# Summing the expert rows of a token block: GpSimd for the first 18 blocks, VectorE for the other 14

## What is computed

```
xn = layernorm(x)
out = x + attention(xn) + ffn(xn)

# ffn: 8 of 64 experts for each token, weighted, and a shared expert
tidx, tw = gate(xn)                      # 8 experts and 8 weights a token
y[t] = sum over k of tw[t,k] * expert[tidx[t,k]](xn[t])
ffn  = y + silu(xn @ Ws_gate) * (xn @ Ws_up) @ Ws_down
```

## Time and profile before

| what | value |
|---|---|
| device time, median of 3 runs | 1333.56 us (1332.71 to 1335.41) |
| profiled execution, its own time | 1338.67 us |
| profiled execution, its span | 1336.9 us |
| mean granted TensorE clock | 0.973 of full speed |
| TensorE (PE) busy | 1255.4 us, 94% |
| VectorE (DVE) busy | 953.3 us, 71% |
| ScalarE (ACT) busy | 861.7 us, 64% |
| GpSimd (POOL) busy | 638.7 us, 48%, nothing from 1000 us on |

### The profile page before, as it was taken

The page is one execution under the profiler, slowest core; times in us unless marked ns, Lnnn a source line. Parts: engine busy times, 40 slices in busy tenths (PEclk is TensorE's granted clock), DMA queues, the critical chain, the costliest instruction groups (busy, mean ns, idle before and its releaser), DMA issues.

```text
span 1336.9 us, 38681 instructions
## 1 busy us (share of the span) xinstructions
PE 1255.4 (94%) x9266; PEld 1182.4 (88%) x9267; DVE 953.3 (71%) x4532; ACT 861.7 (64%) x2383; POOL 638.7 (48%) x747
## 2 busy tenths in 40 slices
PE   4957999999999989999999999999999999999996
PEld 3956999999999979999999999999988999999985
DVE  6776666666666637667676676765559898989897
ACT  2323877777777856556565566566657777777774
POOL 7803777777777726565565665656650000000000
PEclk9678999999999979999999999999999999999998
DMA  8107455544333337777777777775545333333330
GB/s 255 63 1 280 163 185 188 206 163 162 123 118 112 114 120 223 211 233 223 224 232 212 233 226 214 233 215 170 175 139 218 107 106 106 106 109 113 116 119 19
DMA packets 152813, 218.40 MB, mean 163 GB/s; under 512 B 24769, under 2 KB 124866, under 8 KB 147650
## 3 DMA queue, kind: packets, MB, share of 16 engines
q1 hardware_dynamic: 80450, 86.77, 20.4%
q0 software_dynamic: 28800, 86.54, 16.9%
q10 hardware_dynamic: 43520, 44.57, 13.1%
HBM read 113.86 MB, written 103.81 MB: 163 GB/s over the span
## 4 chain that ended last, share of the span: by engine, by line
PE 73%; DVE 12%; issue 6%; DMA 3%; ACTq 2%; ACT 2%; DVEq 1%; SPq 1%
PE psS L951 19%; PE psS L824 10%; PE psT L935 5%; PE psO L960 5%; PE psT L838 4%; PE psM L960 4%; DVE x_all L1604 4%; DMA pr<-slot_rows 2%; PE psQ L771 2%; PE psV L811 2%; PE psV L782 2%; PE psQ L792 2%; PE psT L852 2%; PE psT L851 2%; PE psT L850 1%
## 5 line engine op out<-in xcount | busy, mean ns | idle before, releaser
L951 PEld LDWEIGHTS psS<-sm,wt 128*128 128x128 f32 x2560 | 310.8, 193 | 19.5 <-issue 7.8
L951 PE MATMUL psS<-sm,wt 128*128 128x128 f32 x2560 | 316.6, 277 | 1.7 <-ACT sm L1210 0.7
L636 POOL DMA_INDIRECT slot_rows<-x_out_st,idx_st x256 | 257.0, 1004 | 77.5 <-issue 68.6
L1116 ACT ACTIVATE pr<-sm,nmax 128x192 f32<-128x192 f32 x512 | 205.1, 449 | 54.5 <-DVE nmax L1544 52.7
L824 PE MATMUL psS<-kT,qz 128*128 128x192 f32 x1024 | 225.2, 343 | 10.8 <-DVE qz L1487 8.4
L663 POOL DMA_INDIRECT home_rows<-qz,row_idx x160 | 154.6, 966 | 131.0 <-DVE qz L1637 103.4
L663 POOL DMA_INDIRECT home_rows<-sm,row_idx x160 | 155.3, 971 | 86.4 <-issue 45.0
L1228 ACT COPY wt<-shared_mem 128x512 f32 x320 | 183.4, 627 | 4.8 <-issue 4.8
L1216 ACT ACTIVATE prT<-psS 128x256 f32<-128x256 f32 x160 | 61.6, 385 | 187.7 <-issue 100.0
L824 PEld LDWEIGHTS psS<-kT,qz 128*128 128x128 f32 x1024 | 164.3, 192 | 18.4 <-issue 10.3
L1544 DVE CUSTOM_DVE_ANT_0 sm<-psS,pr 128x192 f32<-128x192 f32 x512 | 162.0, 353 | 18.5 <-issue 14.6
(11 more groups left out here) (283 smaller groups left out, 2492.6 us busy)
## 6 DMA issues: line engine op xcount, KB each, us to landing
shared_mem<-home_rows SPq DMA_DIRECT2D x32, 1024.0 KB, 5.1
pr<-slot_rows ACTq DMA_DIRECT2D x120, 272.0 KB
qz<-slot_rows ACTq DMA_DIRECT2D x40, 272.0 KB
slot_rows<-wt SPq DMA_DIRECT2D x32, 272.0 KB
shared_mem<-in_L_ffn_We_gate SPq DMA_DIRECT2D x64, 128.0 KB
shared_mem<-in_L_ffn_We_up SPq DMA_DIRECT2D x64, 128.0 KB
shared_mem<-in_L_ffn_We_down SPq DMA_DIRECT2D x64, 128.0 KB
x_all<-in_L_attn_x SPq DMA_DIRECT2D x4, 1024.0 KB, 9.1
```

Source lines behind the costliest of these rows:

```text
L636: pool.indirect_dma_start(slot_rows, bass.IndirectOffsetOnAxis(ap=idx_st[:, j, k:k + 1], axis=0), x_out_st[:, j % 2, :], None).then_inc(sc ...
L951: last = mm(psS[:, j % 2, (2 * a + n) * P:(2 * a + n + 1) * P], wt[j % 2][:, a, c, n * F:(n + 1) * F], xsT[:, j % 2, a, c, :], start=(c == ...
L1116: nc.scalar.activation(pr[:, p % 4, par, :], sm[:, p % 4, par, :], ACT.Exp, bias=nmax[:, p % 4, par:par + 1], scale=-1.0).then_inc(probs, 1)
```

## The change

`FIRST` becomes 18, so stage 2 does blocks 0 to 17 and stage 4 does blocks 18 to 31.

Expert rows of blocks 0 to 17 are now summed by GpSimd in stage 4 (`combine_past`), with five instructions a block. The first multiplies the 8 rows (2048 floats a partition) in place by their weights, three additions of 1024, 512 and 256 floats fold them into one, and a last one adds that to `x_all`. All inputs and outputs lie in SBUF. Rows of blocks 18 to 31 stay with VectorE: the body of block i adds the 8 rows of block i itself, one at the end of each step, and in the first body two at the end of each of the last four steps. The `closing` sums are gone. `accumulate` now waits for the block's own expert sum, which the same engine issued before it.

There are five row buffers instead of four, two for GpSimd and three for VectorE. SP's loop is written out: in its step n it waits for VectorE's block n - 1 of this stage, loads VectorE's rows two blocks ahead, tells VectorE of the next block's rows, and then waits for GpSimd's blocks 2n and 2n + 1 in turn, loading GpSimd's next rows and storing the finished block after each.

```diff
-FIRST = NB // 2 + 1
+FIRST = 18
+OWN_ROWS, PAST_ROWS = 3, 2
...
+            def store_past(t):
+                sp.wait_ge(past_combined, t + 1)
+                if t + PAST_ROWS < FIRST:
+                    load_past(t + PAST_ROWS)
+                sp.dma_start(yt[:, t, :], x_all[:, t, :]).then_inc(stored, 16)
+
+            load_past(0)
+            load_own(FIRST)
+            load_past(1)
+            load_own(FIRST + 1)
+            load_own(FIRST + 2)
+            announce_own(FIRST)
+            for n in range(NB - FIRST):
+                t = FIRST + n
+                if n:
+                    sp.wait_ge(combined, n)
+                    if t + 2 < NB:
+                        load_own(t + 2)
+                if t + 1 < NB:
+                    announce_own(t + 1)
+                if n >= 3:
+                    store_own(t - 3)
+                for m in (2 * n, 2 * n + 1):
+                    if m < FIRST:
+                        store_past(m)
...
+            def combine_past(j, t, g):
+                pool.wait_ge(rows_ready[j], 16 * (g + 1))
+                row = rows_in[:, j, :, :]
+                nc.gpsimd.tensor_tensor(row, row, w8[:, t, :].unsqueeze(2).broadcast_to([P, K, D]), ALU.mult).then_inc(past_steps, 1)
+                for n, k in enumerate((K // 2, K // 4, K // 8)):
+                    pool.wait_ge(past_steps, 4 * t + n + 1)
+                    nc.gpsimd.tensor_tensor(row[:, 0:k, :], row[:, 0:k, :], row[:, k:2 * k, :], ALU.add).then_inc(past_steps, 1)
+                pool.wait_ge(past_steps, 4 * t + 4)
+                nc.gpsimd.tensor_tensor(x_all[:, t, :], x_all[:, t, :], row[:, 0, :], ALU.add).then_inc(past_combined, 1)
+
+            pool.wait_ge(weights_kept, 1)
+            pool.wait_ge(acc_done, FIRST)
+            with pool.Fori(0, FIRST // PAST_ROWS) as g:
+                for j in range(PAST_ROWS):
+                    combine_past(j, g * PAST_ROWS + j, g)
...
-                    if closing and s in (1, 2, 5, 7):
-                        n = (1, 2, 5, 7).index(s)
-                        if n == 0:
-                            dve.wait_ge(acc_done, NB - 1)
-                        combine(NB - 2 + n // 2, 2 + n // 2, range(n % 2 * 4, n % 2 * 4 + 4))
-                    if resuming and s >= NPAIR // 2:
-                        for n in range(2):
-                            add_row(i, 4 * s - 2 * NPAIR + n)
-                    if combining:
-                        add_row(i, 2 * s)
...
-                    if resuming and s >= NPAIR // 2:
-                        for n in range(2, 4):
-                            add_row(i, 4 * s - 2 * NPAIR + n)
-                    if combining:
-                        add_row(i, 2 * s + 1)
...
+                    if combining and live and resuming and s >= NPAIR - K // 2:
+                        for k in range(2):
+                            add_row(i, 2 * (s - NPAIR) + K + k)
+                    if combining and live and not resuming:
+                        add_row(i, s)
```

More of the change, by code:

```diff
@@ L118, in build @@
         ring_d = shared_mem[:, RING * 2 * D:RING * WE].rearrange("p (r n) -> p r n", r=RING)
-        rows_in = shared_mem[:, 0:ROWS * K * D].rearrange("p (j k d) -> p j k d", j=ROWS, k=K)
+        rows_in = shared_mem[:].rearrange("p (j k d) -> p j k d", j=OWN_ROWS + PAST_ROWS, k=K)
         gbias = sb("gbias", [P, E])
@@ L340, in build @@
         idx_ready = sem("idx_ready")
-        rows_ready = [sem(f"rows_ready{j}") for j in range(ROWS)]
+        rows_ready = [sem(f"rows_ready{j}") for j in range(OWN_ROWS + PAST_ROWS)]
         rows_landed = sem("rows_landed")
@@ L345, in build @@
         combined = sem("combined")
+        past_steps = sem("past_steps")
+        past_combined = sem("past_combined")
         slot_rows = nc.dram_tensor("slot_rows", (SLOTS + E * P, ROW), F32, kind="Internal").ap()
@@ L469, in _, with load_past, load_own, announce_own @@
                 sp.wait_ge(y_out[j], 32 * (PAIRS // YS))
-            def load_rows(j, t):
+            def load_past(t):
+                sp.dma_start(rows_in[:, t % PAST_ROWS, :, :], home[t]).then_inc(rows_ready[t % PAST_ROWS], 16)
+            def load_own(t):
+                j = PAST_ROWS + t % OWN_ROWS
                 sp.dma_start(rows_in[:, j, :, :], home[t]).then_inc(rows_ready[j], 16)
-            def announce_rows(j, g):
-                sp.wait_ge(rows_ready[j], 16 * (g + 1))
+            def announce_own(t):
+                sp.wait_ge(rows_ready[PAST_ROWS + t % OWN_ROWS], 16 * ((t - FIRST) // OWN_ROWS + 1))
@@ L476, in announce_rows, with store_own @@
                 sp.sem_inc(rows_landed, 1)
-            def store_block(t):
-                sp.wait_ge(combined, t + 1)
+            def store_own(t):
                 sp.wait_ge(acc_done, t + 1)
                 sp.dma_start(yt[:, t, :], x_all[:, t, :]).then_inc(stored, 16)
[L483 to L492, removed]
@@ L493, in _ @@
-            for j in range(ROWS):
-                store_block(NB - ROWS + j)
+            def store_past(t):
[9 more added lines that the diff above has]
+            announce_own(FIRST)
@@ new lines, in _ @@
+            for n in range(NB - FIRST):
[11 more added lines that the diff above has]
+                        store_past(m)
+            for t in range(NB - 3, NB):
+                store_own(t)
@@ L1531, in keep_shared, with accumulate @@
                 v.scalar_tensor_tensor(hs[:], sg[:], 0.5, psQ[:, P:2 * P], ALU.mult, ALU.mult).then_inc(hs_ready, 1)
-            def accumulate(i):
+            def accumulate(i, combining):
                 dve.wait_ge(out_ready, i + 1)
+                if combining:
+                    dve.wait_ge(combined, i - FIRST + 1)
                 v.tensor_tensor(x_all[:, i, :], psV[:, D:2 * D], x_all[:, i, :], ALU.add).then_inc(acc_done, 1)
@@ L1546, in mask_pair, with body @@
                                            nmax[:, p % 4, u:u + 1]).then_inc(masked, 1)
-            def body(i, blk, nth, live=True, tail=True, ahead=True, last_tail=True, combining=False, closing=False, resuming=False):
+            def body(i, blk, nth, live=True, tail=True, ahead=True, last_tail=True, combining=False, resuming=False):
                 if live:
@@ L1553, in body @@
                         mask_pair(i, s, nth)
[L1554 to L1563 removed]
                     if s == 0 and tail and last_tail:
[L1565 removed]
+                        accumulate(i - 2, combining)
                     if s == 1 and live:
@@ L1586, in body, with add_row @@
                         latent_out(i)
-                    if resuming and s >= NPAIR // 2:
-                        for n in range(2, 4):
-                            add_row(i, 4 * s - 2 * NPAIR + n)
-                    if combining:
-                        add_row(i, 2 * s + 1)
[L1594 to L1605, removed]
+                    if combining and live and resuming and s >= NPAIR - K // 2:
[3 more added lines that the diff above has]
+                        add_row(i, s)
+            def add_row(t, k):
+                n = t - FIRST
+                if k == 0:
+                    dve.wait_ge(rows_landed, n + 1)
+                else:
+                    dve.wait_ge(combine_steps, (K - 1) * n + k)
+                row = rows_in[:, bass.ds(PAST_ROWS + t % OWN_ROWS, 1), k, :].rearrange("p a d -> p (a d)")
+                ins = v.scalar_tensor_tensor(x_all[:, t, :], row, w8[:, t, k:k + 1], x_all[:, t, :], ALU.mult, ALU.add)
+                ins.then_inc(combine_steps if k < K - 1 else combined, 1)
             def attention(start, end, combining):
@@ L1614, in attention @@
                     dve.wait_ge(gu_ready, PAIRS)
-                body(start, start % BPS, nth, tail=False, resuming=combining)
+                body(start, start % BPS, nth, tail=False, combining=combining, resuming=combining)
                 body(start + 1, start % BPS + 1, max(nth, 1), last_tail=False, combining=combining)
@@ L1619, in attention @@
                 body(end - 1, (end - 1) % BPS, 2, ahead=False, combining=combining)
[L1620 to L1623, removed]
+                body(end, None, 2, live=False, combining=combining)
+                accumulate(end - 1, combining)
             def make_h(j, u, first):
```

## The result

The changed kernel takes 1402.99 us (median; 1401.31 to 1403.82) against 1334.49 us of the kernel before in the same comparison: 1.0511 times as long, 95% interval 1.0490 to 1.0531. The forecast was 1409 us, in a range of 1355 to 1465. The profiled execution has a span of 1402.0 us and a mean granted TensorE clock of 0.948, against 1336.9 us and 0.973.

A forecast was written before the change was run, and what follows sets the result against it. TensorE was taken to bound stage 2, nearly joined by VectorE in stage 4. Gain -12.8, exclusion +83 and clock +5 us sum to +75 us on 1333.6, so 1409 us, range 1355 to 1465.

The forecast's parts named there:

- The gain, -12.8 us: Stage 4 laid out anew with fewer rows on VectorE, as if GpSimd disturbed nobody: span ends at 1324.1 against 1336.9 us.
- That long instructions shut VectorE out to their end: Stage 4: GpSimd's and VectorE's instructions with two SBUF inputs exclude each other for the whole instruction, even at 4.5 us.
- without exclusion: Rival for stage 4: slack covers exclusion or long instructions let VectorE in; 1321 us, 1320 to 1327; chance 0.09.
- with holds of 1.27 us at most: Rival for stage 4: holds end after 1.27 us, stalls cost +40 us; 1361 us, 1340 to 1380; chance 0.09.
- The size of a stall, 6.6 us a GpSimd block: VectorE in stage 4: five GpSimd instructions, 9.6 us less 0.6 us passing beside each; 119 us for 18 blocks.
- the line through the additions: GpSimd's time estimated from additions of 512 and 256 elements: 2.125 ns an element plus 0.18 us; product 4.53 us.
- The slack of 36 us: Nine VectorE blocks in stage 4, each with 4.0 us of slack against TensorE, taken off the 119 us of stalls.
- the total of +83 us: Stage 4's loss by exclusion: 119 us of stalls less 36 us of slack, as nine blocks of about 30 us.
- The clock, +5 us: TensorE in stage 4's 30 us blocks may fall from 2.4 to 1.2 GHz at times: +5 us, 0 to 36.
- The heavy case (1440 us): Rival for stage 4: exclusion and TensorE's low clock together, +36 us for the clock; up to 1465 us; chance 0.12.
- The queues: SP's new waits for GpSimd stand before VectorE's loads and announcements: free while two GpSimd blocks fit one 30 us VectorE block.
- The sum: Whole kernel: -12.8 + 83 + 5 = +75 us on the median of 1333.6 us, giving 1409 us.

The follow-up runs named there:

- the pieces of 256: The changed kernel with GpSimd's five instructions a block cut into sixteen of 256 elements, same arithmetic: stage 4 took 333.6 us, 1.0059 of the kernel before on its chip.

## Why the prediction was right

**The gain, -12.8 us.** By stage 4 it is -13.2 us. The loop came out at 21.03 us where I took 21.1, and the end at 33.3 us where I took 31.7 + 2.2. The first body of 20.0 us took 21.6 without sums (20.1 with GpSimd only writing), the second 19.2 for 19.7.

**That long instructions shut VectorE out to their end.** Shown: by the product of 3.87 us above, by the kernel with the sums left out, and by the one that only writes. The rivals without exclusion and with holds of 1.27 us at most are both refuted.

**The size of a stall, 6.6 us a GpSimd block.** Too large. In six loop blocks (1080 to 1262 us), with twelve GpSimd blocks, VectorE's held groups took longer than their usual means by 57.2 us, 4.8 us a GpSimd block. They are the rows, in this view of the changed kernel, and some of the small ones.

```profile
L1630 DVE SCALAR_TENSOR_TENSOR x_all<-shared_mem,w,x_all x48 | 66.7, 1390 | 0.1
...
L1524 DVE TENSOR_TENSOR qz<-qT,own_head 128x1024 f32<-128x1024 f32 x12 | 14.6, 1216 | 0.0
...
L1550 DVE SCALAR_TENSOR_TENSOR small<-lmax,small 128x256 f32<-128x256 f32 x6 | 6.6, 1102 | 0.2
L1518 DVE SCALAR_TENSOR_TENSOR small<-dif,remote_z 128x256 f32<-128x256 f32 x6 | 5.1, 854 | 0.2
```

Rows: 48 x (1390 - 479) ns = 43.7 us, the rest 13.5 us. One part of the error is the product: 3.77 us and not the 4.53 of the line through the additions, while the additions of 1024 and 512 took what the line gives (2.41 and 1.38 us). The other is the work that passes meanwhile, which is 0.9 us rather than 0.6 (the sums above). `keep_q` was not held in these blocks (1216 ns), which I had expected; in the kernel without rows it was.

**The slack of 36 us.** This step was wrong. I subtracted VectorE's idle time as a sum, and next to nothing of it was used up: 18 x 4.8 = 86 us of stalls became 84.4 us at the end. Busy time by windows, columns as in the earlier trace rows, shows it directly, first six loop blocks of the changed kernel beside GpSimd, then four without GpSimd's sums.

```profile
1080.00:1262.50 182.50, 151.56 (x931) 141.06 (x930) 156.00 (x428) 99.28 (x323) 107.61 (x60) 0.82 0.30 116
```

```profile
1344.00:1428.00 84.00, 83.18 (x621) 79.38 (x620) 66.60 (x284) 65.63 (x212) 0.00 (x0) 1.00 0.45 169
```

VectorE stands idle for (182.50 - 156.00) / 6 = 4.4 us a block in the one and (84.00 - 66.60) / 4 = 4.4 us in the other. The two kernels with additions in early and late steps show why: of this idle time 3.2 us are waits for scores that work in the first three steps can fill, and holds of up to 3.8 us fell in the later ones too, where TensorE and ScalarE wait for VectorE. The two errors were nearly equal (119 for 86 us, 36 for 2 us), so the total of +83 us is right in part by luck.

**The clock, +5 us.** TensorE's clock did fall, to 0.66 to 0.93 in stretches of 20 us beside GpSimd, but no cost of it could be shown. The heavy case (1440 us) did not come.

**The queues.** As forecast they cost nothing: VectorE waited 1.2 us in all for announced rows, and GpSimd 73.9 us for its loads, as SP holds it to VectorE's pace. The first two blocks are longer, since SP did not hold GpSimd back yet and six of its blocks fell in them. I had expected four in the first; it was between two and three.

**The sum.** -13.2 + 84.4 = +71.2 us. Measured were +68.5 and, with the changed kernel run again, 1404.47 - 1333.26 = +71.2 us. The spans of the two profiled executions differ by 65.1 us only: stage 2 begins at 114.6 us in that of before, and at 106.4 to 108.7 us in those of the changed kernel and the three others on the chip of 1333.26 us. The profiled execution of before was 5.1 us over its median, which fits that in size; no run shows the reason.

No version with the whole sum is faster than the kernel before. The nearest, the pieces of 256, is at 1.0059 (1.0029 to 1.0089). The gain of taking rows off VectorE is 13.2 us by stage 4, and the cheapest form of GpSimd's sums that was run costs 28.3.

## What to carry to other kernels

Before work goes to GpSimd beside a busy VectorE, count on both sides the instructions that read SBUF twice: each long one on GpSimd held the next such one on VectorE to its end, whatever data it touched, and the price went by the length of the instruction over what VectorE had to do meanwhile (0.7 to 0.9 us here), and not by busy time. Cut in pieces of that size, the same work cost a third. And idle time of an engine that others wait for is slack only in the step where it lies: add up a stall and the idle time of the same step, not of the whole block.

## What the runs showed of the hardware

- GpSimd's product with a weight that is the same along 256 elements takes 3.77 us for 2048, its addition of 1024 takes 2.41 us: 1.8 and 2.4 ns an element with all overhead. A fill of 2048 takes 1.81 us.
- A GpSimd that only fills, for 9.0 us a block, leaves VectorE's two-input instructions at their usual length, and holds a 128x384 copy for 0.26 us and a one-input instruction of 128x16 for 0.66 us in the mean.
- `mask_pair`, with one input in SBUF and one in PSUM, stayed at 350 ns beside GpSimd's sums.
- Two chips took some 250 us longer for the kernel before (1584.6 and 1588.0 for 1334.5 us). On both of them the loop in stage 2, with GpSimd's indirect transfers in it, took some 28 us a block instead of 21, and a block of stage 4 without GpSimd's sums took the same 21.0 us. Why wasn't looked into.
